# Layer 1's experts as one stream of 71 row slots over all eight batches, in a two-layer attention and expert kernel

## The chip, the core and the metric

The kernel runs on one core of a Trainium2 chip. A core has five engines that run their own instruction lists side by side and wait for each other through semaphores: PE (matrix multiply, with its weight loads shown apart as PEld), DVE (vector), ACT (scalar and activation), POOL (general), and SP, which here only issues DMAs. Work on chip lies in SBUF (128 partitions) and in PSUM, eight banks in which PE leaves its results. The metric is the time of one execution in microseconds, median over the runs.

## The reference, cut to what matters

The input is eight batches of 512 rows of 128 numbers. Each of two layers adds causal attention with 16 heads and then a layer of eight experts:

```
x = x + attention0(layernorm(x))
x = x + experts0(layernorm(x))      # each row goes to 1 of 8 experts
x = x + attention1(layernorm(x))
x = x + experts1(layernorm(x))      # each row goes to 2 of 8 experts

def experts1(x):                    # w1[e]: 128 x 512, w2[e]: 512 x 128
    probs = softmax(x @ gate_w.T + gate_b)
    vals, idx = top_k(probs, 2)
    return sum(vals[k] * (relu(x @ w1[idx[k]] + b1[idx[k]]) @ w2[idx[k]] + b2[idx[k]]) for k in (0, 1))
```

## The kernel before

**Sorted rows and slots.** Rows are not computed with all eight experts. DVE finds for each row its expert and a place in a DRAM table (`route`, `choose`, `places`), POOL sends the rows there by indirect DMAs of one tile of 128 rows each (`scatter`, L1099), and the table is then read in tiles of 128 rows that belong to one expert. Such a tile is a **slot**. For each slot SP loads the expert's `w1` (`fetch_w1`, L943) and the rows (`fetch`), PE turns the rows (`turn_rows`, L1308) and multiplies twice (`first`, L1331, with the ReLU on ACT, and `second`, L1341), and DVE adds the bias into a buffer `kept` (its row reads `w<-psum,w_now`). In layer 1 POOL then sends the finished tile to a DRAM tensor `returned`, each row to the place of its token (`send`, L1107). At the end SP reads `returned` (`take_back`, L997), two loads of 128x512 a batch, since a row has two experts; ahead of the first batch of each group it passes 32 waits, one for each buffer of `kept`, until that half's sends are all done (L992); DVE multiplies them by the gates and adds them to X (`add`, L1555, four instructions of one 128x128 tile each); and SP stores the batch (L1007). Batch 5's adds are on ACT and POOL.

**Groups and halves.** `GROUPS_OF` splits the batches of a layer into groups that are routed together: in layer 1 batches 0 to 3, 4 and 5, 6, and 7. Since experts do not fill their last tile, a table that is closed needs up to 7 slots more than it has tiles of rows. Before the change each half (batches 0 to 3, and 4 to 7) has a table of its own. The first half is one group of 32 + 7 = 39 slots, read in plain order with one DMA for four tiles (L976). The second half is a **stream** of three groups with 9, 8 and 22 slots: a group takes only tiles that are surely full, the last takes the rest, and each tile's place is read from a table `tile_at` at run time, with one DMA a tile (L972). Before the last group's rows are read, the step `tail` (L952) writes eight blocks of empty rows behind the experts' ends. Layer 1 has 78 slots in all.

**Order.** The order of steps on every engine is a table of letters, `ORDERS`, one string an engine, a letter for a kind of step; the PSUM bank of each PE step is a digit of `BANKS`. Attention is split into steps too: `max` (PE L1213 and L1219, then DVE's row maximum, L1524), `score` (PE L1239, the exponential on ACT, and for blocks on the diagonal a mask on POOL, L1088), `values` (L1257). Expert slots and attention steps of the next batches are mixed in these lists. Each engine takes its list strictly in order, so a step that waits holds all behind it. `w1` buffers are a ring of six: SP's load for slot n waits until the `second` of slot n - 6 has been read. The rows' buffers are a ring of two, four tiles each.

## Time and profile before

| | |
|---|---|
| median of 3 runs | 961.92 us (958.96 to 962.04) |
| the profiled execution | 958.88 us |
| its span in the profile | 957.0 us |
| PE busy | 856.2 us |
| PE weight loads busy | 572.6 us |
| DVE busy | 669.4 us |
| ACT busy | 609.4 us |
| POOL busy | 533.2 us |
| TensorE's mean granted clock | 0.963 of full speed |

The span is from the first to the last instruction that the profiler shows; the execution's own time is 1.88 us longer. Busy times overlap, since the engines run side by side; what counts is which engine ends last in each stretch.

### The profile page before, as it was taken

Reading aid. Unit: us, or ns where it says so; the run is one execution under the profiler, and the core shown is the slowest. Engines: PE = TensorE matmul, PEld = TensorE weight load, DVE = VectorE, ACT = ScalarE, POOL = GpSimd, SP = SyncE. Lnnn points to the kernel's source line nnn. Section 1 sums busy time; section 2 is a strip of 40 time slices with the busy share of each in tenths; the row PEclk is TensorE's granted clock in tenths of the full one; section 3 lists DMA queues with packets and bytes.
Section 4 is the critical chain, followed back from the end, with each engine's and each line's share of the span. In section 5 each row is a group of like instructions: output and inputs, shape, how many; then the busy total and the mean of one; then the engine's idle time right before and its main releaser. Section 6 shows DMA issues by size and latency. Waiting matters only on the chain.

```text
span 957.0 us, 24622 instructions
## 1 busy us (share of the span) xinstructions
PE 856.2 (89%) x8968; PEld 572.6 (60%) x8968; DVE 669.4 (70%) x1379; ACT 609.4 (64%) x1173; POOL 533.2 (56%) x809
## 2 busy tenths in 40 slices
PE   3689999989999899988999999999799997899991
PEld 1334455434999445434998444454445597799990
DVE  1889899788545899887567899789999537111117
ACT  3077889865444588685434696788578864555661
POOL 3043544557000588677203787567788775687452
PEclk9999999989999899979999999799899999999996
DMA  5625642444674436341984517435441256778786
GB/s 142 155 83 128 172 112 75 74 113 148 197 223 147 118 113 156 87 135 54 304 255 129 130 54 160 128 78 120 122 124 36 77 167 184 227 228 252 237 247 207
DMA packets 137312, 141.14 MB, mean 147 GB/s; under 512 B 35564, under 2 KB 113452, under 8 KB 137100
## 3 DMA queue, kind: packets, MB, share of 16 engines
q1 hardware_dynamic: 130604, 126.04, 47.4%
q0 software_dynamic: 6592, 13.55, 4.4%
q8 instruction: 74, 1.21, 0.5%
q14 instruction: 42, 0.34, 0.1%
HBM read 98.73 MB, written 44.36 MB: 150 GB/s over the span
## 4 chain that ended last, share of the span: by engine, by line
PE 36%; DVE 9%; issue 3%; DMA 2%; ACT 2%; SPq 0%; POOL 0%; DVEq 0%; ACTq 0%; POOLq 0%
PE psum L1331 11%; PE psum L1341 9%; PE psum L1257 5%; DVE neg_max L1524 4%; PE psum L1239 2%; PE psum L1213 2%; DMA rows_in<-sorted_in 1%; ACT scratch L1453 1%; PE psum L1308 1%; PE psum L1219 1%; PE psum L1283 1%; DVE route L1521 1%; PE psum L1175 1%; DVE X L1555 1%; DMA w<-sorted_out,rows_of 1%
## 5 line engine op out<-in xcount | busy, mean ns | idle before, releaser
L1524 DVE TENSOR_REDUCE neg_max<-psum 128x2 f32<-128x768 f32 (+3 forms) x352 | 379.6, 1119 | 41.0 <-PE psum L1219 38.7
L1453 ACT ACTIVATE scratch<-psum 128x1024 f32<-128x1024 f32 x320 | 316.1, 1022 | 80.4 <-PE psum L1239 77.9
L1088 POOL TENSOR_SCALAR_AFFINE_SELECT scratch<-scratch 128x512 f32<-128x512 f32 x256 | 158.5, 641 | 124.3 <-ACT scratch L1453 123.2
L1331 PE MATMUL psum<-rows_t,w_now 128*128 128x128 f32 x1360 | 169.5, 277 | 5.9 <-issue 3.8
L1257 PE MATMUL psum<-scratch,values 128*32 128x512 f32 (+3 forms) x2048 | 170.0, 452 | 1.7 <-POOL scratch L1088 0.8
L1331 PEld LDWEIGHTS psum<-rows_t,w_now 128*128 128x128 f32 x1360 | 159.7, 193 | 10.4 <-issue 7.4
L1213 PE MATMUL psum<-k_stack,q_stack 52*128 52x128 bf16 (+3 forms) x1024 | 133.2, 321 | 17.8 <-DVE neg_max L1524 7.9
L1341 PE MATMUL psum<-w,hidden_t 128*128 x992 | 131.3, 279 | 5.1 <-ACT hidden_t L1490 1.7
L1239 PE MATMUL psum<-q_stack,k_stack 55*128 55x512 bf16 (+3 forms) x1024 | 121.9, 312 | 12.7 <-DVE neg_max L1524 7.1
L1490 ACT ACTIVATE hidden_t<-psum,w_now 128x128 f32<-128x128 f32 x312 | 88.6, 373 | 60.6 <-PE psum L1331 46.3
L1341 PEld LDWEIGHTS psum<-w,hidden_t 128*128 128x128 f32 x992 | 119.7, 193 | 10.2 <-issue 10.0
L1099 POOL DMA_INDIRECT sorted_in<-xn_half,rows_of x96 | 94.1, 980 | 33.4 <-issue 20.8
L1213 PEld LDWEIGHTS psum<-k_stack,q_stack 52*128 52x128 bf16 x1024 | 43.8, 98 | 96.1 <-issue 39.0
L1521 DVE TENSOR_TENSOR w<-psum,w_now 128x128 f32<-128x128 f32 x78 | 22.7, 291 | 109.1 <-PE psum L1341 107.8
L1107 POOL DMA_INDIRECT returned<-w,goes_to x78 | 76.8, 985 | 37.9 <-issue 19.0
L1219 PE MATMUL psum<-masks_bf 64*128 64x64 bf16 (+2 forms) x1408 | 93.0, 211 | 0.0
L1257 PEld LDWEIGHTS psum<-scratch,values 128*32 128x32 f32 x2048 | 55.1, 111 | 62.1 <-issue 40.6
L1219 PEld LDWEIGHTS psum<-masks_bf 64*128 64x128 bf16 x1408 | 70.6, 101 | 30.9 <-issue 4.9
L1239 PEld LDWEIGHTS psum<-q_stack,k_stack 55*128 55x128 bf16 x1024 | 36.4, 96 | 73.1 <-issue 31.7
L1778 DVE SCALAR_TENSOR_TENSOR hidden_t<-w,psum 128x512 f32<-128x512 f32 x46 | 31.6, 687 | 58.2 <-PE psum L1341 33.0
L1070 POOL TENSOR_TENSOR rot<-rot 128x512 f32<-128x512 f32 x16 | 20.4, 1272 | 50.0 <-DVE rot L1521 49.9
L1078 POOL TENSOR_TENSOR max_parts<-max_rest,max_parts 32x128 bf16<-32x128 f32 x32 | 13.5, 422 | 57.3 <-ACT max_parts L1349 57.1
(141 smaller groups left out, 1007.2 us busy)
## 6 DMA issues: line engine op xcount, KB each, us to landing
w_now<-in_w SPq DMA_DIRECT2D x78, 322.0 KB
w_now<-in_w SPq DMA_DIRECT2D x46, 512.0 KB, 4.4
q_stack<-q_parts SPq DMA_DIRECT2D x64, 192.0 KB, 4.2
q_parts<-q_parts SPq DMA_DIRECT2D x16, 384.0 KB, 2.9
k_stack<-k_parts SPq DMA_DIRECT2D x32, 192.0 KB, 3.7
q_parts<-q_parts SPq DMA_DIRECT2D x16, 256.0 KB, 2.9
w<-in_w SPq DMA_DIRECT2D x16, 256.0 KB, 4.4
scratch<-returned SPq DMA_DIRECT2D x16, 256.0 KB, 4.0
```

Of the source, the lines that this page charges most:

```text
L1088: pool.affine_select(out=diag, in_=diag, compare_op=ALU.is_ge, fill=0.0, base=0, pattern=[[0, 4], [1, P]], channel_multiplier=-1).then_inc ...
L1099: pool.indirect_dma_start(sorted_in[s.layer][half_of(s.layer, g)][:, :], bass.IndirectOffsetOnAxis(ap=row_of(s.layer, g, t, k), axis=0), x ...
L1107: pool.indirect_dma_start(returned[h][:, :], bass.IndirectOffsetOnAxis(ap=goes_to[h][:, j:j + 1], axis=0), kept[slot], None).then_inc(sent ...
L1213: pe.matmul(out[:, j * width:(j + 1) * width], q_stack[i][rows, pair, t * P:(t + 1) * P], k_stack[i][rows, k_of(layer, pair), 0:width], st ...
L1219: ins = pe.matmul(blocks, ident_of[half, :], mask[half, :].unsqueeze(1).to_broadcast([P // 2, n, P // 2]), start=False, stop=(first > widt ...
L1239: ins = pe.matmul(bank[u.bank + k][:, off:off + SEQ - j * P], k_stack[i][rows, k_of(layer, pair), j * P:(j + 1) * P], q_stack[i][rows, pai ...
L1257: ins = pe.matmul(bank[u.bank][CW * c:CW * c + CW, j * P:SEQ], values[batch_of(s) % 3][:, j, col:col + CW], p[:, c % 2, off:off + SEQ - j ...
L1331: ins = pe.matmul(bank[v.bank][:, c * P:(c + 1) * P], w1_now[layer][w.slot][:, n * FFN + c * P:n * FFN + (c + 1) * P], rows)
L1341: ins = pe.matmul(bank[u.bank][:, 0:P], hidden_t[h.slot][:, k * P:(k + 1) * P], w2[layer][:, bass.ds(e, 1), k * DIM:(k + 1) * DIM].rearran ...
L1453: act.activation(expd[s.slot], psum[:, u.bank:u.bank + 2, :], ACT.Exp, scale=SCALE).then_inc(read[u.bank], 1)
L1490: ins = act.activation(hidden_t[s.slot][:, c * P:(c + 1) * P], bank[u.bank][:, c * P:(c + 1) * P], ACT.Relu, bias=w[:, FFN + c:FFN + c + 1])
L1524: return dve.tensor_reduce(out=out, in_=in_, axis=AX, op=op, negate=negate)
```

## The change

All of layer 1 is one stream: the helpers `half_of`/`of_half` give way to `stream_of`, `of_stream` and `same_stream`, which put all four groups of layer 1 in stream 0. The groups now have 25, 16, 8 and 22 slots, 71 in all instead of 78. There is one table `sorted_in` for layer 1, with regions of 8 batches and a tile for each expert, one `returned`, one `goes_to`, `expert_of` and `tile_at`. The first group's rows are now found through `tile_at` too, and only the last group has a tail. The token number that travels with each row gets an offset for the half (L1712 before). The wait of the first `take_back` is for the sends of the whole stream. `rotate` on PE gets an explicit wait. Layer 0 computes and sorts as before. `ORDERS` and `BANKS` are new from the first letter to the last, for all five engines and both layers; the banks of single steps may now be odd ones too.

```diff
     return GROUPS_OF[layer][g][0] // GB
-def of_half(layer, half):
-    return [g for g in range(len(GROUPS_OF[layer])) if half_of(layer, g) == half]
+def stream_of(layer, g):
+    return 0 if layer else half_of(layer, g)
+def of_stream(layer, n):
+    return [g for g in range(len(GROUPS_OF[layer])) if stream_of(layer, g) == n]
+def same_stream(layer, g):
+    return of_stream(layer, stream_of(layer, g))
 def streams(layer, g):
-    return len(of_half(layer, half_of(layer, g))) > 1
+    return len(same_stream(layer, g)) > 1
 def is_final(layer, g):
-    return g == of_half(layer, half_of(layer, g))[-1]
+    return g == same_stream(layer, g)[-1]
 def slots_done(layer, g):
-    tiles = QT * TOPK[layer] * (GROUPS_OF[layer][g][-1] + 1 - half_of(layer, g) * GB)
+    tiles = QT * TOPK[layer] * (GROUPS_OF[layer][g][-1] + 1 - GROUPS_OF[layer][same_stream(layer, g)[0]][0])
     return tiles + (EXPERTS - 1) * (1 if is_final(layer, g) else -1)
 def slots_in(layer, g):
-    same = of_half(layer, half_of(layer, g))
-    return slots_done(layer, g) - (slots_done(layer, g - 1) if g > same[0] else 0)
-def slots_of_half(layer, half):
-    return sum(slots_in(layer, g) for g in of_half(layer, half))
+    return slots_done(layer, g) - (slots_done(layer, g - 1) if g > same_stream(layer, g)[0] else 0)
+def slots_of(layer, n):
+    return sum(slots_in(layer, g) for g in of_stream(layer, n))
 def first_slot(layer, g):
-    return sum(slots_in(layer, k) for k in of_half(layer, half_of(layer, g)) if k < g)
+    return sum(slots_in(layer, k) for k in same_stream(layer, g) if k < g)
 SLOTS = tuple(tuple(slots_in(layer, g) for g in range(len(GROUPS_OF[layer]))) for layer in range(2))
 MAXSLOTS = max(max(ns) for ns in SLOTS)
 HALVES = BATCHES // GB
+STREAMS = (HALVES, 1)
 EPS = 1e-5
 SCALE = float(HD) ** -0.5
 NEG = -3.0e38
...
-C_ID, C_FIRST, C_ONE, C_RANK, C_THR, C_SLOT, C_HALF = 0, 128, 256, 264, 272, 288, 328
-C_TOKEN = 332
+C_ID, C_FIRST, C_ONE, C_RANK, C_THR, C_SLOT = 0, 128, 256, 264, 272, 288
+C_HALF = C_SLOT + MAXSLOTS
+C_TOKEN = C_HALF + QT
...
-RETURNED = 2 * GT * P
-
-REGION = GB * SEQ + P
+RETURNED = HALVES * 2 * GT * P
+
+REGION = BATCHES * SEQ + P
...
 ORDERS = {
...
-        goes_to = [sb(f"goes_to{h}", [P, slots_of_half(1, h)], I32) for h in range(HALVES)]
-        expert_of = [sb(f"expert_of{h}", [1, slots_of_half(1, h)], I32) for h in range(HALVES)]
-        tile_at = sb("tile_at", [1, slots_of_half(1, 1)], I32)
+        goes_to = sb("goes_to", [P, slots_of(1, 0)], I32)
+        expert_of = [[sb(f"expert_of{layer}{n}", [1, slots_of(layer, n)], I32) for n in range(STREAMS[layer])] for layer in range(2)]
+        tile_at = sb("tile_at", [1, slots_of(1, 0)], I32)
...
-        sorted_rows = {(layer, h): EXPERTS * REGION + SPARE * P if len(of_half(layer, h)) > 1 else slots_of_half(layer, h) * P
-                       for layer in range(2) for h in range(HALVES)}
-        sorted_in = [[dram(f"sorted_in{layer}{h}", (sorted_rows[layer, h], widths[layer])) for h in range(HALVES)] for layer in range(2)]
+        sorted_rows = {(layer, n): EXPERTS * REGION + SPARE * P if len(of_stream(layer, n)) > 1 else slots_of(layer, n) * P
+                       for layer in range(2) for n in range(STREAMS[layer])}
+        sorted_in = [[dram(f"sorted_in{layer}{n}", (sorted_rows[layer, n], widths[layer])) for n in range(STREAMS[layer])] for layer in range(2)]
-        returned = [dram(f"returned{h}", (RETURNED + slots_of_half(1, h) * P, DIM)) for h in range(HALVES)]
+        returned = dram("returned", (RETURNED + slots_of(1, 0) * P, DIM))
...
                             sp.wait_ge(tails_set, EXPERTS * DMA)
-                        tiles = sorted_in[s.layer][half_of(s.layer, s.b)].rearrange("(n p) d -> n p d", p=P)
+                        tiles = sorted_in[s.layer][stream_of(s.layer, s.b)].rearrange("(n p) d -> n p d", p=P)
                         found = values_at(tile_at, first_slot(s.layer, s.b) + 4 * s.x, n, EXPERTS * REGION_TILES + SPARE - 1)
...
-                        for slot, value in enumerate(sends_made(of_half(1, half_of(1, g))[-1])):
+                        for slot, value in enumerate(sends_made(same_stream(1, g)[-1])):
-                        first = (k * GT + QT * x) * P
-                        sp.dma_start(taken_back(b, k), returned[half_of(1, g)][first:first + QT * P, :].rearrange("(p t) d -> p t d", p=P)
+                        first = ((2 * half_of(1, g) + k) * GT + QT * x) * P
+                        sp.dma_start(taken_back(b, k), returned[first:first + QT * P, :].rearrange("(p t) d -> p t d", p=P)
...
-                    pool.indirect_dma_start(sorted_in[s.layer][half_of(s.layer, g)][:, :], bass.IndirectOffsetOnAxis(ap=row_of(s.layer, g, t, k), axis=0),
+                    pool.indirect_dma_start(sorted_in[s.layer][stream_of(s.layer, g)][:, :], bass.IndirectOffsetOnAxis(ap=row_of(s.layer, g, t, k), axis=0),
-                    h, j = half_of(1, g), first_slot(1, g) + s.x
-                    pool.indirect_dma_start(returned[h][:, :], bass.IndirectOffsetOnAxis(ap=goes_to[h][:, j:j + 1], axis=0),
+                    j = first_slot(1, g) + s.x
+                    pool.indirect_dma_start(returned[:, :], bass.IndirectOffsetOnAxis(ap=goes_to[:, j:j + 1], axis=0),
...
                 elif s.kind == "rotate":
+                    x = of("turn", 1, b, "xn")
+                    pe.wait_ge(read[x.uses[0].bank], x.uses[0].after)
                     room(u)
                     pe.matmul(bank[u.bank], (wq1, wq1_sw)[s.y][:, :], xt[of("turn", 1, b, "xn").slot][:, :]).then_inc(full[u.bank], 1)
 
...
-                        dve.tensor_copy(xn_half[:, mine, DIM], consts[:, C_TOKEN + mine.start:C_TOKEN + mine.stop])
+                        dve.tensor_scalar(xn_half[:, mine, DIM], consts[:, C_TOKEN + mine.start:C_TOKEN + mine.stop],
+                                          float(half_of(1, g) * 2 * GT * P), None, ALU.add, ALU.bypass)
...
-                        base, ends = (region if g == of_half(layer, half_of(layer, g))[0] else e_small[:, 4, :]), e_small[:, 3, :]
+                        base, ends = (region if g == same_stream(layer, g)[0] else e_small[:, 4, :]), e_small[:, 3, :]
...
-                    dve.tensor_copy(expert_of[half_of(layer, g)][:, j:j + ns], slot_f[:, 0:ns]).then_inc(experts_known, 1)
+                    dve.tensor_copy(expert_of[layer][stream_of(layer, g)][:, j:j + ns], slot_f[:, 0:ns]).then_inc(experts_known, 1)
```

Three places of the new orders follow; in each the first list is before the change, the second after it. Line numbers after the change are 10 to 13 higher.

**PE at the start.** L1145, L1153, L1159 and L1161 (after: L1155 to L1171) are the turn, q and k/v products of one batch; L1213 and L1219 (L1225 and L1231) begin batch 0's row maxima.

```order
L1145 MATMUL psum<-consts,xn 128x128 x4
L1153 MATMUL psum<-xn_t,wq 128x512
L1159 MATMUL psum<-xn_t,wkv 32x128 x4
L1161 MATMUL psum<-wkv,xn_t 128x32 x4
L1213 MATMUL psum<-k_stack,q_stack 128x128 x8
L1219 MATMUL psum<-masks_bf 128x4x64 x4
L1213 MATMUL psum<-k_stack,q_stack 128x256 x4
L1219 MATMUL psum<-masks_bf 128x2x64 x4
```

```order
L1155 MATMUL psum<-consts,xn 128x128 x4
L1163 MATMUL psum<-xn_t,wq 128x512
L1169 MATMUL psum<-xn_t,wkv 32x128 x4
L1171 MATMUL psum<-wkv,xn_t 128x32 x4
L1155 MATMUL psum<-consts,xn 128x128 x4
L1163 MATMUL psum<-xn_t,wq 128x512
L1169 MATMUL psum<-xn_t,wkv 32x128 x4
L1171 MATMUL psum<-wkv,xn_t 128x32 x4
L1225 MATMUL psum<-k_stack,q_stack 128x128 x8
L1231 MATMUL psum<-masks_bf 128x4x64 x4
```

Batch 2's turn and products now stand ahead of the first row maximum; before, two batches did.

**POOL in the attention of batch 7.** AFFINE_SELECT (L1088, after: L1098) is the mask of a score block; the DMA to `sorted_in` (L1099, after: L1109) scatters rows of layer 1's group 1, the DMA to `returned` (L1107, after: L1117) sends a finished tile of group 0. The last AFFINE_SELECT of each list is the last of batch 7.

```order
L1088 AFFINE_SELECT scratch<-scratch 128x4x128 x9
L1099 DMA sorted_in<-xn_half,rows_of 18304x129 x2
L1088 AFFINE_SELECT scratch<-scratch 128x4x128 x4
L1043 TENSOR_TENSOR ln_small<-ln_small,consts 128x4
L1044 TENSOR_TENSOR ln_small<-ln_small,consts 128x4
L1046 TENSOR_TENSOR ln_small<-ln_small,consts 128x4
L1048 TENSOR_TENSOR ln_small<-ln_small 128x4
L1088 AFFINE_SELECT scratch<-scratch 128x4x128 x3
```

```order
L1109 DMA sorted_in<-xn_half,rows_of 34688x129
L1098 AFFINE_SELECT scratch<-scratch 128x4x128
L1117 DMA returned<-w_0,goes_to 17280x128 x2
L1042 TENSOR_TENSOR route_small<-consts 128x4
L1109 DMA sorted_in<-xn_half,rows_of 34688x129
L1117 DMA returned<-w_0,goes_to 17280x128
L1098 AFFINE_SELECT scratch<-scratch 128x4x128 x2
L1109 DMA sorted_in<-xn_half,rows_of 34688x129 x2
L1098 AFFINE_SELECT scratch<-scratch 128x4x128
```

Before, two scatters of group 1 stood ahead of the last masks. Now, with rows ahead of those shown, 11 scatters and 5 sends stand between group 1's first scatter and the last mask.

**DVE at the end.** w2_0<-psum,w1_now (L1521, after: L1533) takes a finished slot out of PSUM; the SCALAR_TENSOR_TENSOR of L1555 (after: L1567) is `add`, and its gate names the half and the expert of the two, `gate01` the first half's second.

```order
L1555 SCALAR_TENSOR_TENSOR X<-scratch,gate00,X 128x128 x4
L1521 TENSOR_TENSOR w2_0<-psum,w1_now 128x128
L1555 SCALAR_TENSOR_TENSOR X<-scratch,gate01,X 128x128 x4
L1555 SCALAR_TENSOR_TENSOR X<-scratch,gate00,X 128x128 x4
L1555 SCALAR_TENSOR_TENSOR X<-scratch,gate01,X 128x128 x4
L1555 SCALAR_TENSOR_TENSOR X<-scratch,gate00,X 128x128 x4
L1555 SCALAR_TENSOR_TENSOR X<-scratch,gate01,X 128x128 x4
L1555 SCALAR_TENSOR_TENSOR X<-scratch,gate00,X 128x128 x4
L1555 SCALAR_TENSOR_TENSOR X<-scratch,gate01,X 128x128 x4
L1555 SCALAR_TENSOR_TENSOR X<-scratch,gate10,X 128x128 x4
L1555 SCALAR_TENSOR_TENSOR X<-scratch,gate11,X 128x128 x4
```

```order
L1533 TENSOR_TENSOR w2_0<-psum,w1_now 128x128 x13
L1567 SCALAR_TENSOR_TENSOR X<-scratch,gate00,X 128x128 x4
L1567 SCALAR_TENSOR_TENSOR X<-scratch,gate01,X 128x128 x4
L1567 SCALAR_TENSOR_TENSOR X<-scratch,gate00,X 128x128 x4
L1567 SCALAR_TENSOR_TENSOR X<-scratch,gate01,X 128x128 x4
L1567 SCALAR_TENSOR_TENSOR X<-scratch,gate00,X 128x128 x4
L1567 SCALAR_TENSOR_TENSOR X<-scratch,gate10,X 128x128 x4
L1567 SCALAR_TENSOR_TENSOR X<-scratch,gate01,X 128x128 x4
L1567 SCALAR_TENSOR_TENSOR X<-scratch,gate00,X 128x128 x4
L1567 SCALAR_TENSOR_TENSOR X<-scratch,gate10,X 128x128 x8
L1567 SCALAR_TENSOR_TENSOR X<-scratch,gate11,X 128x128 x8
L1567 SCALAR_TENSOR_TENSOR X<-scratch,gate01,X 128x128 x4
L1567 SCALAR_TENSOR_TENSOR X<-scratch,gate11,X 128x128 x4
```

Before, one add stood ahead of the last slot and the adds followed in the order of batches, 14 in all. Now all 14 stand behind the last slot, and the sixth, the first with `gate10`, is batch 6's. On SP all sixteen loads of L997 (after: L1007) now stand behind the last load of a `w1`, by order of batch; before, the first half's eight were issued by themselves, two of them ahead of the last two `w1`.

## Rows read from the trace of the kernel before

**Rows 1.** The page of the run before: span and PE

```profile
span 957.0 us, 24622 instructions
...
PE 856.2 (89%) x8968; PEld 572.6 (60%) x8968; DVE 669.4 (70%) x1379; ACT 609.4 (64%) x1173; POOL 533.2 (56%) x809
```

**Rows 2.** Windows: busy us of PE, PEld, DVE, ACT, POOL; clock, DMA share, GB/s

```profile
675.00:700.00 25.00, 19.92 (x247) 11.05 (x240) 24.16 (x34) 12.14 (x18) 18.98 (x24) 0.86 0.57 157
775.00:850.00 75.00, 65.39 (x538) 62.22 (x537) 30.97 (x151) 40.45 (x136) 51.35 (x73) 0.98 0.70 210
840.00:920.00 80.00, 77.48 (x673) 75.43 (x672) 13.87 (x51) 50.23 (x171) 52.86 (x75) 1.00 0.78 232
```

**Rows 3.** Matmuls of three lines from 840 to 920 us, ns min/median/max

```profile
L1331 PE MATMUL psum<-rows_t,w_now x317: 275/275/349, 840.3 to 920.0; 128*128 128x128 f32 x159
...
L1341 PE MATMUL psum<-w,hidden_t x317: 274/275/372, 839.8 to 919.2; 128*128 x159
...
L1308 PE MATMUL psum<-consts,rows_in x39: 272/273/300, 849.4 to 919.4; 128*128 128x128 f32 x39
```

**Rows 4.** The chain from 934 us to the end: start, us, what

```profile
937.35 2.43 DMA returned<-w,goes_to
...
940.57 0.32 SPq L997
...
941.88 0.43 SPq L997
...
943.73 0.32 SPq L997
...
944.10 3.15 DMA scratch<-returned
...
953.23 0.52 DVE X L1555 x2
```

**Rows 5.** The timeline from 930 us: start, us, instruction

```profile
935.11 1.15 PE L1341 MATMUL psum<-w,hidden_t 128*128 x8 [0.42 <-ACT hidden_t L1490]
...
936.50 10.29 DVE L1555 SCALAR_TENSOR_TENSOR X<-scratch,gate,X 128x128 f32<-128x128 f32 x36
```

**Rows 6.** The timeline of PE, ACT and DVE in the first 60 us

```profile
19.36 1.11 PE L1145 MATMUL psum<-consts,xn 128*128 128x128 f32 x4 [2.06 <-ACT xn L1412]
...
23.77 1.92 PE L1161 MATMUL psum<-wkv,xn_t 128*128 128x32 f32 x8
27.98 0.61 PE L1213 MATMUL psum<-k_stack,q_stack 52*128 52x128 bf16 x8 [2.29 <-issue]
...
17.67 1.64 ACT L1412 ACTIVATE xn<-X,ln_small 128x128 f32<-128x128 f32 x4
...
23.29 0.60 ACT L1349 ACTIVATE q_parts<-psum 128x512 bf16<-128x512 f32 x1 [2.18 <-PE psum L1153]
...
49.76 0.85 DVE L1579 BATCH_NORM_STATS2 ln_small<-X 128x6 f32<-128x128 f32 x4
50.64 0.38 DVE L1582 BATCH_NORM_AGGREGATE ln_small<-ln_small 128x2 f32<-128x6 f32 x4
```

**Rows 7.** The timeline of DVE in the routing of layer 1's group 1

```profile
748.33 0.48 DVE L1753 SCALAR_TENSOR_TENSOR jump<-taken,e_small 1x8 f32<-1x8 f32 x1
...
750.97 0.22 DVE L1524 TENSOR_REDUCE route<-route 1x9 f32<-1x72 bf16 x1
```

**Rows 8.** The timeline of POOL, two indirect DMAs four apart

```profile
764.31 1.00 POOL L1099 DMA_INDIRECT sorted_in<-xn_half,rows_of  x1 [0.16 <-issue]
...
769.62 1.00 POOL L1099 DMA_INDIRECT sorted_in<-xn_half,rows_of  x1 [0.16 <-issue]
```

**Rows 9.** The timeline of SP and DVE: tail step and one row fetch

```profile
819.89 10.20 SPq L952 DMA_DIRECT2D sorted_in<-in_empty_rows  x8
...
897.36 2.23 SPq L972 DMA_DIRECT2D rows_in<-sorted_in  x4
...
902.16 0.35 DVE L1538 CAST goes_to<-rows_in 128x4 int32<-128x4 f32 x1 [1.37 <-DMA rows_in<-sorted_in]
```

92 lines of the change are left out of this document (46 added, 46 removed).

## The prediction

> **What bounds the kernel now.** I read the page first: PE is busy 856.2 of a span of 957.0 us [rows 1]. Such an average mixes stages, so the windows come next [rows 2]. From 675 to 700 us, in layer 1's attention, DVE is busy 24.16 of 25 us and PE 19.92: the row maxima and the routing end last there. From 840 to 920 us only expert slots run: PE is busy 77.48 of 80 us, its weight loads 75.43, DVE 13.87 and POOL 52.86, so PE alone bounds it. Between them, from 775 to 850 us, PE is idle 75.00 - 65.39 = 9.61 us while the last groups are routed. Last, the chain and the timeline of the end: the last matmuls begin at 935.11 and take 1.15 us [rows 5], so PE ends at 936.26 and 20.7 us of the span follow with PE idle. There the order is last send, 32 waits, take-back, add, store [rows 4]. The kernel is thus bound by three things in turn, and the change touches each.
>
> **The slots that are gone.** From 840 to 920 us the trace has 317 + 317 matmul instructions of L1331 and L1341 [rows 3]. A slot has eight of each (four products, each in two passes), so this is 634 / 16 = 39.6 slots, or 80 / 39.6 = 2.02 us a slot, with its share of turned rows (39 tiles, L1308). Seven slots less are 7 x 2.02 = 14.1 us. They are PE's full price only where PE ends last; all of layer 1's slots but the first few lie in such stretches, so I take 14.1. ACT, DVE, POOL (seven sends) and SP (seven loads of w1) lose work too, which lay beside PE's: nothing for it. The bound from below, if half of it fell in a stage where PE waits for others, is 7.0.
>
> **The end.** I count from L, the landing of the last send. Before, L is 937.35 + 2.43 = 939.78, that is 3.5 us after PE's end [rows 4, 5]. Nothing changes up to there: POOL's last sixteen sends follow their slots one by one in both orders.
> Before, the first half's adds ran while the last send was under way: DVE did 36 instructions in 10.29 us from 936.50 [rows 5], 0.286 us each, 1.14 us an add. Only 32 semaphore waits, four loads, 32 waits again and batch 6's load stand between L and the rest: the first load is issued at 940.57 (0.8 after L), the fourth ends at 942.31, so a load costs SP 0.44 to 0.47; 32 waits take until 943.73, 1.4 us; that load lands at 944.10 + 3.15 = 947.25 [rows 4].
> After, all adds wait for L, since the one `returned` is complete only then. SP: rest of the waits 1.1 (25 instead of 18 of the 32 stand behind the last one), eight loads 3.7, waits 1.4, four loads 1.8, waits 1.4: batch 6's first load is issued at L + 9.4 and lands 3.5 later, at L + 12.9. DVE begins at about L + 4.6 and would have done five adds by L + 10.3, but its sixth is batch 6's: it stands still for 2.6 us. Then nine adds are left, 9 x 1.14 = 10.3, to L + 23.2. The last store takes as now, from 953.75 (the end of the last add) to 957.0, 3.3 us [rows 1, 4]. The end is at L + 26.5 instead of L + 17.2: **+9.3 us**. If DVE's sixth add cost no wait it would be +6.7; if the transfers (16 loads and 8 stores of 256 KB, 6.3 MB) ran at the mean 232 GB/s of the slot stage [rows 2] they would take 27 us instead of the 22 that I give them, so +14.
>
> **The start.** PE's list has batch 2's turn and products ahead of the first row maximum. For batch 1 this group runs from 19.36 to 23.77 + 1.92 = 25.69, 6.3 us. Batch 2's needs its normalised rows; ACT makes them in 1.64 us behind the q copy that ends at 23.89, so at 25.5. PE would reach the first maximum at about 32.0 instead of 27.98 [rows 6]: +4.0. DVE's list in turn has the statistics of batches 2, 3 and 4 ahead of the maxima, in its idle time; each costs 0.85 + 0.38 = 1.2 us now inside the stretch of maxima [rows 6], so -3.7. PE's 6.3 us for batch 2 are also not due later. I take 0 for the start: between +4.0 (nothing paid back) and -2.3 (both engines' work is worth its full length: 4.0 - 6.3).
>
> **Routing group 0 as a stream.** The extra operations are those of group 1 now: from 748.33 to 750.97, 2.6 us of small instructions on DVE [rows 7]; the others replace such as are dropped. For group 0 they fall in the stage that DVE bounds, where a stall of DVE makes the next maximum late and with it PE. Between 0 (a wait for PE near by swallows it) and 2.6, I take 1.4. The offset of the token and PE's new wait cost nothing: the first is one small instruction instead of another, the second waits for a copy that the latent product of the same batch waits for.
>
> **Row fetches and fills.** Group 0's rows now take four DMAs a fetch and a load of table entries: SP spends 2.23 us on four [rows 9] where one DMA of 256 KB stood. SP is mostly idle in that stage; 0. Five fills of the old padding slots fall away, in DMA time that nothing waits for; 0. The eight tail DMAs, 10.20 us on SP [rows 9], are there before and after, once each, with w1 loads behind them.
>
> **Sum.** -14.1 + 9.3 + 0 + 1.4 = -3.4 us. Against the profiled execution's own 958.88 us this is 955.5. The median of the runs shown is 961.92, 3.0 above that execution, and the sum does not depend on which of them is taken: **958.5 us** for the median. All other parts of the lists are new as well, in both attentions; of these I can't price single moves, and they carry the width of the range. What a measurement can't tell from no change is about 0.3%, 2.9 us: 959.0 to 964.8.
>
> **The rivals.**
> (a) *The re-ordered attention is better packed* (0.17). DVE and PE start the maxima with batch 2's work done, and both bounds of the start hold in full: -2.3, and DVE's added routing falls into a wait, 0. With the end at +6.7: -14.1 + 6.7 - 2.3 = -9.7, 952.2 us. For it: PE idles anyway between 25.69 and 27.98 [rows 6]; against it: a stretch like that of 675 to 700 is already full on DVE [rows 2].
> (b) *POOL makes batch 7's masks late*, the slower side (0.20). Between group 1's first scatter and batch 7's last mask POOL had 2 indirect DMAs and now has 16. Four indirect DMAs take 769.62 - 764.31 = 5.3 us, 1.33 each [rows 8]; 14 more are 18.6 us. What covers it is PE's own list: batch 7's last product now has 14 slots ahead instead of 5, 9 x 2.02 = 18.2 us of PE work. Cover and delay are equal, so any slot that comes late shows. It decides (slower by more than 2.9) once 6.3 us of the 18.6 are uncovered; with half of them, -3.4 + 9.3 = +5.9, 967.8 us. One would see PE wait on POOL's `scratch` in the values of batch 7.
> (c) *Rows come late* (0.18). Fewer slots stand between the last routing and its first rows, 24 instead of 39, and the first `turn_rows` of group 3 only 16 slots, 32 us, behind its `places`. The fetch at 897.36 landed by 902.16, 4.8 us [rows 9]; in three places the new PE list leaves only four to five products of 0.9 us between a freed row buffer and the next turn from it. Each may stall 1 to 2 us: -3.4 + 4 = +0.6, 962.5 us. The Trainium skill (DMA: Bandwidth & Descriptors, Bandwidth) speaks against single tiles too: it says to batch DMAs to 1 MiB or more and gives 0.95 us for 64 KB. By this page four tiles occupy the DMA engines for 3.8 us, an estimate from its figure, which in a stage where they are busy 0.78 of the time would make rows later still; no run here shows a 64 KB transfer alone.
> (d) *The slots bring less*: with -7.0 for them, +3.7, 965.6 us; part of (b) in its effect, and small (0.05).
>
> **How the numbers follow.** My forecast has 0.40, with a range of its own from 954.5 to 962 (the bounds 0 to 2.6, -2.3 to +4.0 and the end's +6.7 to +14 don't all go one way). Faster by over 0.3%: (a) and 0.31 of the forecast's 0.40, together 0.48. Within: 0.09 of the forecast, (c), and little of (b): 0.29. Slower: most of (b), (d): 0.23. The range takes in (a) with some room, and (b)'s half-covered case: 950 to 968.
>
> **What would show it.** Right: 14 x 8 fewer matmul instructions on the two slot lines; PE's last matmul some 12 us earlier, near 924; after it 30 us with PE idle, in them DVE waiting about 2.6 us behind its fifth add for a load, and 56 add instructions behind the last slot; the first maximum at 32 us. Wrong: the first matmul of group 0 at another distance from the end of layer 0 than now, which would be the attention's lists; PE waits on POOL masks late in batch 7 (b); waits of L1320 on rows (c); loads landing at less than 300 GB/s in the end, which would make it DMA's and not DVE's.

## The result: the change makes the kernel slower

984.54 us median (980.74 to 990.64, 4 runs) stand against 961.98 before (4 runs): a ratio of 1.0256, 95% interval [1.0209, 1.0303]. I had forecast 958.5 us in a range of 950 to 968. The profiled execution took 990.64 us, the longest of the four, so its trace shows some 6 us more loss than the median.

First the page of the changed kernel (span, busy time, granted clock by slices, one group):

```profile
span 988.6 us, 24399 instructions
...
PE 862.2 (87%) x8849; PEld 572.1 (58%) x8849; DVE 672.0 (68%) x1381; ACT 601.9 (61%) x1143; POOL 525.1 (53%) x792
...
PEclk9999999998999989999999999998898999979995
...
L1343 PE MATMUL psum<-rows_t,w_now 128*128 128x128 f32 x1304 | 168.0, 283 | 14.2 <-DMA w_now<-in_w 12.3
```

119 matmuls are gone, 17 for each of the seven slots (8968 before, [rows 1]), and PE is still 6 us longer busy. Then windows of the changed kernel: window, length, busy us of each engine (instructions), clock, DMA share, GB/s:

```profile
0.00:50.00 50.00, 31.19 (x205) 17.86 (x207) 25.47 (x67) 17.95 (x44) 15.83 (x37) 1.00 0.69 154
675.00:700.00 25.00, 20.74 (x207) 8.39 (x205) 23.52 (x57) 17.00 (x23) 15.21 (x21) 0.84 0.62 143
840.00:920.00 80.00, 64.38 (x489) 61.47 (x490) 15.02 (x66) 34.77 (x117) 47.19 (x66) 0.91 0.68 194
845.00:895.00 50.00, 37.92 (x270) 36.19 (x270) 7.40 (x33) 19.20 (x66) 26.80 (x37) 0.86 0.65 185
```

The third row answers to the last of [rows 2]: the stretch in which PE alone was the bound (77.48 of 80 us) has lost 13 us of PE's work. What PE waits for shows in its waits over the whole span (us in total, times, longest):

```profile
PE psum L1343 <- DMA w_now<-in_w: 12.3, 7, 3.6
...
PE psum L1251 <- DMA q_stack<-max_parts_out: 10.1, 7, 2.8
...
PE psum L1320 <- DMA rows_in<-sorted_in: 4.5, 3, 2.9
```

L1251 are the scores of attention, which wait for the row maxima on their way through DRAM. In the kernel before, the same list has no wait of the first two kinds, and 0.3 us of the third. Behind the first stands SP's queue. Its timeline in group 1's slots (start, us from first to last issue, line, count):

```profile
842.97 5.84 SPq L982 DMA_DIRECT2D rows_in<-sorted_in  x8
849.04 3.45 SPq L953 DMA_DIRECT2D w_now<-in_w  x3
853.65 1.88 SPq L982 DMA_DIRECT2D rows_in<-sorted_in  x4
855.72 1.17 SPq L953 DMA_DIRECT2D w_now<-in_w  x2
858.09 5.31 SPq L982 DMA_DIRECT2D rows_in<-sorted_in  x8
864.67 1.37 SPq L953 DMA_DIRECT2D w_now<-in_w  x3
866.90 9.74 SPq L962 DMA_DIRECT2D sorted_in<-in_empty_rows  x8
```

Last the end, to be read against [rows 4, 5]: last products, last send, loads, and the adds of DVE:

```profile
956.28 1.15 PE L1353 MATMUL psum<-w,hidden_t 128*128 x8 [0.43 <-ACT hidden_t L1502]
...
958.52 0.96 POOL L1117 DMA_INDIRECT returned<-w,goes_to  x1 [0.58 <-issue]
961.11 10.09 SPq L1007 DMA_DIRECT2D scratch<-returned  x16
964.44 2.38 DVE L1567 SCALAR_TENSOR_TENSOR X<-scratch,gate,X 128x128 f32<-128x128 f32 x8 [6.68 <-DMA scratch<-returned]
...
973.61 11.62 DVE L1567 SCALAR_TENSOR_TENSOR X<-scratch,gate,X 128x128 f32<-128x128 f32 x36 [3.08 <-DMA scratch<-returned]
```

PE ends at 957.43 and 31.2 us follow; I had said 30. DVE stands still once more, 3.08 us (I had said 2.6).

To see where the rest went I matched PE's matmuls with the steps of its list and took the end of the same step in each profile; for a slot this is the end of its first product (`first`). This is worked out from the trace's records, not a view of it. Slots are numbered 0 to 70 in the new order; the seven that are gone stood between slots 31 and 32. The columns between the first and the last are kernels of the experiments below:

```
end of the step, us           before  old_lists  start_new  cut_250  cut_380_again  front_new   after
first row maximum, batch 0      29.0       29.2       32.9     32.7           33.0       32.8    32.8
layer 0, group 0, slot 22      305.9      304.5      307.9    309.2          314.8      318.9   318.3
layer 0, group 1, slot 22      522.1      518.8      523.2    521.1          533.9      540.6   538.8
layer 1, slot 0                756.0      754.5      763.4    758.1          769.6      781.3   771.1
slot 16                        801.8      803.1      809.3    804.8          817.9      827.2   821.3
slot 31                        841.4      848.4      852.0    850.1          861.0      871.6   862.2
slot 41                        874.9      869.8      875.4    873.0          883.7      894.0   895.5
last product                   936.3      931.4      936.8    934.4          945.0      955.3   957.4
end of the span                957.0      959.8      966.2    962.3          972.9      983.2   988.6
```

The changed kernel's 31.6 us are thus: 15.1 up to slot 0 (both attentions and layer 0), 5.7 more to slot 31, -0.2 to slot 41 (where seven slots less should have given 10 or more), 0.6 behind it, and 10.5 at the end. One profile each stands behind these numbers. Through layer 0 PE, ACT, DVE and POOL have the same lists in before and in old_lists, and still the two differ by 1.4 and 3.3 us in the two rows of layer 0, so a difference of 3 us in one row says little. The sign that I had named for a loss in attention, another distance from the end of layer 0 to slot 0, looks at the wrong place: it is 233.9 us before and 232.3 after. The loss is already there at the end of layer 0, 16.7 us against before and 20.0 against old_lists.

### The profile page after: what moved, and what is told of

Its sections match the earlier page's. It is cut to its first block, busy times and chain, and to the rows that moved or that the text cites. A ratio compares the mean times of both kernels' runs of the same rounds, so it can differ in the third digit from the quotient of the medians.

```text
span 988.6 us, 24399 instructions
## 1 busy us (share of the span) xinstructions
PE 862.2 (87%) x8849; PEld 572.1 (58%) x8849; DVE 672.0 (68%) x1381; ACT 601.9 (61%) x1143; POOL 525.1 (53%) x792
## 4 chain that ended last, share of the span: by engine, by line
PE 45%; DVE 16%; DMA 11%; issue 8%; POOL 7%; SPq 7%; ACT 6%; DVEq 0%; ACTq 0%; POOLq 0%
PE psum L1343 11%; DVE neg_max L1536 9%; PE psum L1353 8%; PE psum L1269 7%; PE psum L1225 4%; PE psum L1251 4%; ACT scratch L1465 4%; DMA rows_in<-sorted_in 2%; DMA max_parts_out<-max_parts 2%; SPq L982 2%; POOL scratch L1098 2%; DMA w_now<-in_w 2%; POOL sorted_in L1109 2%; DMA q_stack<-max_parts_out 2%; PE psum L1231 1%
## 5 line engine op out<-in xcount | busy, mean ns | idle before, releaser
L1098 POOL TENSOR_SCALAR_AFFINE_SELECT scratch<-scratch 128x512 f32<-128x512 f32 x256 | 160.0, 644 | 173.9 <-ACT scratch L1465 173.0
L1343 PE MATMUL psum<-rows_t,w_now 128*128 128x128 f32 x1304 | 168.0, 283 | 14.2 <-DMA w_now<-in_w 12.3
L1269 PE MATMUL psum<-scratch,values 128*32 128x512 f32 (+3 forms) x2048 | 174.6, 462 | 2.9 <-POOL scratch L1098 1.1
L1343 PEld LDWEIGHTS psum<-rows_t,w_now 128*128 128x128 f32 x1304 | 157.2, 197 | 20.6 <-issue 10.2
L1225 PE MATMUL psum<-k_stack,q_stack 52*128 52x128 bf16 (+3 forms) x1024 | 132.2, 320 | 19.1 <-DVE neg_max L1536 9.3
L1251 PE MATMUL psum<-q_stack,k_stack 55*128 55x512 bf16 (+3 forms) x1024 | 119.9, 311 | 19.5 <-DMA q_stack<-max_parts_out 10.1
L1353 PE MATMUL psum<-w,hidden_t 128*128 x936 | 126.9, 286 | 5.7 <-ACT w L1361 3.0
L1353 PEld LDWEIGHTS psum<-w,hidden_t 128*128 128x128 f32 x936 | 116.7, 199 | 11.2 <-issue 10.4
L1502 ACT ACTIVATE hidden_t<-psum,w_now 128x128 f32<-128x128 f32 x284 | 80.4, 373 | 62.2 <-PE psum L1353 37.9
L1109 POOL DMA_INDIRECT sorted_in<-xn_half,rows_of x96 | 94.1, 980 | 32.1 <-issue 20.6
L1117 POOL DMA_INDIRECT returned<-w,goes_to x71 | 69.6, 980 | 47.7 <-DVE w L1533 29.8
L1231 PE MATMUL psum<-masks_bf 64*128 64x64 bf16 (+2 forms) x1408 | 92.4, 210 | 0.0
L1225 PEld LDWEIGHTS psum<-k_stack,q_stack 52*128 52x128 bf16 x1024 | 43.0, 97 | 84.0 <-issue 28.8
L1231 PEld LDWEIGHTS psum<-masks_bf 64*128 64x128 bf16 x1408 | 70.4, 100 | 31.6 <-issue 7.0
L1251 PEld LDWEIGHTS psum<-q_stack,k_stack 55*128 55x128 bf16 x1024 | 37.3, 96 | 85.6 <-issue 26.1
L1533 DVE TENSOR_TENSOR w<-psum,w_now 128x128 f32<-128x128 f32 x71 | 20.0, 289 | 83.2 <-PE psum L1353 83.2
L1088 POOL TENSOR_TENSOR max_parts<-max_rest,max_parts 32x128 bf16<-32x128 f32 x32 | 13.4, 420 | 70.6 <-ACT max_parts L1361 70.3
L1493 ACT ACTIVATE w<-psum 128x512 f32<-128x512 f32 x46 | 27.4, 595 | 29.1 <-DVE hidden_t L1791 18.6
```

The source lines that it names most:

```text
L1098: pool.affine_select(out=diag, in_=diag, compare_op=ALU.is_ge, fill=0.0, base=0, pattern=[[0, 4], [1, P]], channel_multiplier=-1).then_inc ...
L1109: pool.indirect_dma_start(sorted_in[s.layer][stream_of(s.layer, g)][:, :], bass.IndirectOffsetOnAxis(ap=row_of(s.layer, g, t, k), axis=0), ...
L1117: pool.indirect_dma_start(returned[:, :], bass.IndirectOffsetOnAxis(ap=goes_to[:, j:j + 1], axis=0), kept[slot], None).then_inc(sent_back[ ...
L1225: pe.matmul(out[:, j * width:(j + 1) * width], q_stack[i][rows, pair, t * P:(t + 1) * P], k_stack[i][rows, k_of(layer, pair), 0:width], st ...
L1231: ins = pe.matmul(blocks, ident_of[half, :], mask[half, :].unsqueeze(1).to_broadcast([P // 2, n, P // 2]), start=False, stop=(first > widt ...
L1251: ins = pe.matmul(bank[u.bank + k][:, off:off + SEQ - j * P], k_stack[i][rows, k_of(layer, pair), j * P:(j + 1) * P], q_stack[i][rows, pai ...
```

## Experiments

The program of the change and its lists of steps can be parted: the lists of before, with the seven slots taken out, drive the new program as well. All kernels were timed beside the kernel before on the same chip.

**1 to 3. Program or lists?** PE's list begins so in the two:

```diff
 ORDERS["pe"], after -> old_lists
-&ef&ef&efjjjjj&jjjjjjj&ljjjjjjjjpppjjjppljjp...
+&ef&efjjjjjjjjjjjjjljjjjjjjjjppppppjjlj&jjpep...
```

> The program of the change (one stream of 71 slots, one taking back at the end) with the lists and banks of the kernel before: seven slots of the first half's end are left out of them, its taking back and adds are moved behind the last slot in the order of the batches, everything else stands where it stood. Nothing of the computation changes. Theory A, the new lists are what costs: the stretch up to the last slot is as before less seven slots (-14), the end is as in the changed kernel or somewhat longer (+9 to +12), so 956 to 962 us. Rival B, the stream itself costs (all row fetches of group 1 by address on SP, w1 late behind them): the 16 to 18 us that the changed kernel loses between 845 and 895 us show here too, 972 to 980 us. Rival C, both by halves: 963 to 971 us.

> The changed kernel with the old lists (and banks) for all steps that the kernel before had done by 560 us: layer 0 with its experts, and layer 1's attention up to the scores of batch 2. Behind that stand the new lists. Theory A1, the first part of the lists loses what the milestones show there (first product +7, last slots of layer 0 +15 to +17): 968 to 971 us. Rival A2, what the front loses is waited away later, behind the experts' weights and rows: 978 to 984 us.

> The other half of the exchange: the new lists for all steps that the changed kernel had done by 577 us, and behind them the old lists less seven slots, with the taking back and the adds at the end. Theory A1 with additive parts: old_lists plus 13 to 16 us, so 970 to 977 us. Rival A2, the front's delay is hidden later: within 4 us of old_lists. Rival B, the stream on SP costs whatever the lists: 980 us or more.

Measured: old_lists 962.77 us, 1.0036 [0.9995, 1.0078]; front_old 976.86, 1.0144 [1.0069, 1.0219]; front_new 985.11, 1.0242 [1.0158, 1.0326]. The one stream with the old lists costs or gives nothing that can be told; the new lists cost the rest, about 22 us at the medians. The parts don't add: the new first part alone costs all of it, the new second part alone 14. Once the first part is new, the second parts are level in the table (the changed kernel begins its slots 10 us earlier than front_new and takes 12 us longer for them). So neither A1 nor A2 stands as I wrote it. The 985.11 lies where rival B of front_new put it, but old_lists rules B out: the same stream on SP is there too.

**4. A cheaper tail step under the new lists.**

```diff
-                        at = sp.value_load(ends_at[0:1, e:e + 1], ...)
+                        if e % LOADED == 0:
+                            found = values_at(ends_at, e, LOADED, EXPERTS * REGION - P)
+                        at = found[e % LOADED]
```

> The changed kernel, with the eight addresses of the tail step taken by two loads of four values in place of eight loads of one. In the profile of the changed kernel that step holds SP for 9.7 us (1.2 us for each of its eight transfers); two loads at 1.0 us and eight issues at 0.5 us make it 6 us. Theory S, SP bounds the stretch from 840 to 895 us: -3 to -4 us, so 980 to 982 us, and the PE's waits for w1 in 866 to 884 us go from 6.6 to under 4 us. Rival, SP's queue isn't the bound there: no change, 983 to 986 us.

Measured: 986.84 us, 1.0226 [1.0138, 1.0314]: no gain. In its timeline the step is as much shorter as meant, but PE's waits between 845 and 915 us have only changed their name:

```profile
866.20 6.01 SPq L964 DMA_DIRECT2D sorted_in<-in_empty_rows  x8
```

```profile
PE psum L1322 <- DVE w L1535: 7.7, 2, 5.6
PE psum L1345 <- DMA w_now<-in_w: 4.1, 4, 3.2
PE psum L1322 <- DMA rows_in<-sorted_in: 1.9, 1, 1.9
```

L1322 is `turn_rows`: rows are late where weights were. By the chain SP waits there for the last scatter's landing, until 880.5 us, with all its loads behind it. That this is the cause was read, not tried.

**5. The tail step spread, with the old lists.** In old_lists PE loses 5.7 us between slots 16 and 31 (1.3 behind before, then 7.0). SP's timeline, of before and then of old_lists, and a wait of PE in old_lists between 797 and 860 us:

```profile
817.24 0.42 SPq L976 DMA_DIRECT2D rows_in<-sorted_in  x1
```

```profile
816.31 1.88 SPq L982 DMA_DIRECT2D rows_in<-sorted_in  x4
...
826.70 9.80 SPq L962 DMA_DIRECT2D sorted_in<-in_empty_rows  x8
```

```profile
PE psum L1343 <- DMA w_now<-in_w: 4.4, 1, 4.4
```

Four tiles by address cost SP 1.9 us, and 0.9 for the load of their addresses (tail_two's chain), where one transfer of 0.4 us stood. The tail step starts 6.8 us later than in before ([rows 9]: 819.89), and the weights behind it are late. The wait is not all new: at the same place PE stood 3.0 us in before, with no releaser in the profile. Of the 5.7 us 3.6 are waiting (10.3 us from slot 16 to slot 31 instead of 6.7) and the rest longer matmuls, 9.1 us of them at the lower granted clock instead of 3.4.

```diff
+                if tails and s.kind == "fetch_w1" and s.x % 2:
+                    set_tail(sorted_in[1][0])      # one load, one transfer
```

> The one-stream program with the lists of before (old_lists), and the tail step's eight loads and transfers no longer in one piece: one of them goes ahead of every second fetch of w1. SP issues as much as it did, only not all at once. In old_lists that step holds SP for 9.8 us from 826.7 us, w1 lands late behind it (PE waits 4.4 us at L1343) and slots 25 to 28 lose 5.7 us against before. Theory S, SP is where the stream loses: 4 to 6 us less than old_lists, so 957 to 959 us, and that wait goes. Rival, another wait stands behind it (rows of group 1): 961 to 963 us.

Measured: 965.53 us, 1.0076 [1.0047, 1.0106]: no gain, and above what both theories gave. Its profile is of the fastest run (960.76). Slot 31 comes 4.9 us earlier there than in old_lists (843.5), slot 41 not at all (869.9).

**6. Less issued, not only spread.** old_two has the edits of experiments 5 and 4 together.

> old_spread (the one-stream program with the lists of before, the tail step's transfers one ahead of each second fetch of w1), and now with the eight addresses of that step taken by two loads of four values. Spreading alone moved PE's waits about and left slot 41 where it was: the sum of what SP issues was the same. This takes about 4 us of it away between 826 and 862 us. Theory S, in group 1's slots the sum of SP's issues is the bound: PE 3 to 4 us earlier from slot 41 on than in old_spread, so 960 to 962 us. Rival, the sum isn't the bound, the rows of the last batches are: as old_spread, 964 to 966 us.

> old_two once more (the one-stream program with the lists of before, the tail step spread, its addresses by two loads); its first run fell in the hour in which every kernel took 8% longer, and stood at 1.0082 of before. Theory S, the sum of SP's issues is the bound in group 1's slots: PE 3 to 4 us earlier than old_lists from slot 41 on, 959 to 962 us. Rival: as old_lists and old_spread, 963 to 966 us.

Measured: 1.0082 [1.0045, 1.0119] in the first run, where before took 1040.67 us; then 960.41 us beside 959.46, 1.0023 [0.9996, 1.0050]. In its profile slot 41 ends at 865.3, 4.6 us earlier than in old_spread, and the last product at 926.8 (931.2). From slot 16 to slot 41 it takes 61.7 us, old_spread 65.5 and old_lists 66.7. That speaks for theory S, that what SP no longer issues comes back, and the two ratios, 1.0076 and 1.0023, are apart as well. Two things hold it back. Against old_lists no gain shows in the times: 0.9 us above before in both, and the profile of old_two_again is that of its fastest run (956.39). And SP is not issuing all the time: between 826 and 870 us it waits 7.7 us for others there, 8.4 in old_spread and 6.7 in old_lists. So the sum of SP's issues is a large part of the bound in these slots; that it is all of it isn't shown.

**7 to 9. Where do the new lists lose?** start_new, cut_250 and cut_380 take the new lists up to 60, 246 and 380 us; front_new did up to 577.

> old_lists, with the new lists for what the changed kernel had done by 60 us and the old ones behind: only the start is new (batch 2's turn, products and copies ahead of the first maxima). My prediction priced the start at 0 between -2.3 and +4.0. If it is 0: 961 to 964 us. If the first maxima's 3.8 us are never made good: 966 to 967 us. If the start alone carries the loss of the front: 975 us or more.

> old_lists, with the new lists for what the changed kernel had done by 246 us (attention of the first four batches) and the old ones behind. In front_new, where the new lists reach to 577 us, PE stood some 10 us behind old_lists at this point by equal work, and 18 to 24 us at 577 us. Theory, the loss is made before the experts of group 0 and kept: 972 to 976 us. Rival, it is made in layer 0's experts and the attention beside them (250 to 577 us): 962 to 966 us. Rival, the joint itself costs: 980 us or more.

> old_lists, with the new lists for what the changed kernel had done by 380 us and the old ones behind. New lists up to 246 us cost 3 us, up to 577 us 22 us. Theory, many small waits, spread over the stretch: +6 to +13 us over cut_250, so 972 to 979 us. Rival A, one place before 380 us makes all of it: 983 us or more. Rival B, one place behind it (layer 0's group 1 and its experts): 965 to 969 us.

> cut_380 once more, for the same reason. Theory of many small waits: 972 to 979 us; one place ahead of 380 us: 983 us or more; one place behind it: 965 to 969 us.

Measured: start_new 966.70 us, 1.0065 [1.0043, 1.0088]; cut_250 966.23, 1.0071 [1.0043, 1.0100]; cut_380 1.0149 [1.0091, 1.0207] beside the 1040.67, then 979.57, 1.0221 [1.0172, 1.0270]. The start costs about 4 us by the medians of start_new and old_lists, 3 by their ratios (the intervals just overlap), and is not made good; the attention of the first four batches adds nothing to it; the great part, near 19 us by front_new, is made between 250 and 577 us. cut_380 lies in the middle, but its profile has 5 us of waiting near 375 us where its two lists join, so it does not tell many small waits from one place cleanly. Windows of cut_250 and then of front_new:

```profile
245.00:270.00 25.00, 25.00 (x222) 24.26 (x221) 12.12 (x19) 9.42 (x19) 2.17 (x5) 1.00 0.73 216
...
345.00:370.00 25.00, 24.12 (x278) 13.61 (x274) 22.45 (x52) 21.66 (x35) 21.74 (x36) 1.00 0.57 141
```

```profile
245.00:270.00 25.00, 22.31 (x181) 20.61 (x180) 13.95 (x25) 7.56 (x18) 2.39 (x6) 0.86 0.58 185
...
345.00:370.00 25.00, 22.74 (x227) 11.34 (x229) 19.49 (x32) 17.99 (x31) 20.29 (x31) 0.86 0.15 48
```

PE is busy 2.7 and 1.4 us less in these windows of front_new, and their granted clock is 0.86 instead of 1.00. The same time is not the same work in the two, so the rows show only that the two go together. The kind of wait that grows is that of the scores for the maxima's way through DRAM; over the whole span, cut_250 and then front_new:

```profile
PE psum L1251 <- DMA q_stack<-max_parts_out: 5.5, 3, 3.0
```

```profile
PE psum L1251 <- DMA q_stack<-max_parts_out: 10.1, 6, 3.3
```

These 4.6 us are a small part of the 19, and cut_250's own 5.5 (start_new has 1.1) cost nothing that shows in its time. How the rest comes about stands under "What the waits set off".

**10 and 11. The end by itself.** before_late moves the first half's loads, adds and stores behind the last slot in the kernel before. before_wait also lets them wait for the last send of all:

```diff
-                        for slot, value in enumerate(sends_made(of_half(1, half_of(1, g))[-1])):
+                        for slot, value in enumerate(sends_made(len(SLOTS[1]) - 1)):
```

> The kernel before (two streams, 78 slots, its own lists), only that the first half's rows are taken back, added and stored behind the last slot, with the other half's. My prediction put the end at +9.3 us for this; the profiles showed +7.8 (old_lists) and +10.5 us (the changed kernel) between PE's last product and the end. Theory, the end is that price by itself: 969 to 972 us. Rival, the first half's loads and adds also cost PE something where they stood, and their leaving gives it back: 963 to 967 us.

> before_late (two streams, the first half taken back behind the last slot; 959 us), and now the first half's taking back also waits for the last send of all, as it must in one stream. Theory E, the end of one stream is dear since all sixteen transfers start only when the last send has landed, not since sixteen adds stand there: +6 to +8 us over before_late, so 965 to 967 us, and 28 us between PE's last product and the end in place of 21. Rival, the adds' place alone: within 2 us of before_late.

> before_wait once more, for the same reason. Theory E: 965 to 967 us (6 to 8 over before_late), 28 us between PE's last product and the end. Rival: within 2 us of before_late (959).

Measured: before_late 958.95 us, 0.9984 [0.9963, 1.0006], far from my 969 to 972; before_wait 1.0104 [1.0034, 1.0174] beside the 1040.67, then 965.54 us, 1.0065 [1.0045, 1.0085], as theory E said. Loads and adds in before_late, then in before_wait_again:

```profile
924.13 18.60 SPq L997 DMA_DIRECT2D scratch<-returned  x16
...
933.06 18.20 DVE L1555 SCALAR_TENSOR_TENSOR X<-scratch,gate,X 128x128 f32<-128x128 f32 x56
```

```profile
945.51 10.48 SPq L997 DMA_DIRECT2D scratch<-returned  x16
948.88 18.16 DVE L1555 SCALAR_TENSOR_TENSOR X<-scratch,gate,X 128x128 f32<-128x128 f32 x56 [7.19 <-DMA scratch<-returned]
```

The 56 instructions take 18.2 us in both. In the first the rows are there when the last slot leaves (PE ends at 932.8, 21.2 us follow); in the second DVE stands 7.2 us for the first load (PE ends at 941.4, 28.4 follow). The end of one stream is dear through what the transfers wait for, not through the number of adds behind the last slot.

**12. The spread tail step under the new lists.**

> The changed kernel with the tail step's transfers spread: one ahead of each fetch of w1, what is left ahead of the last group's first fetch of rows. In the changed kernel slots 32 to 41 lose 11 to 12 us against old_lists. Theory S as in old_spread (the sum of SP's issues binds, not their place): no change beyond 3 us, 982 to 987 us. Rival, the block of 9.7 us itself makes those slots late: 973 to 978 us.

> new_spread once more: in its first run every kernel, the kernel before too, took 8% longer, and it stood at 1.0076 of before. Theory P, the block of the tail step is what makes slots 32 to 41 late under the new lists: 972 to 979 us, 8 to 12 us less than after_again. Theory S, only the sum of SP's issues counts: within 3 us of after_again.

> The changed kernel once more, as the measure for new_spread on the same chip and hour: 981 to 988 us where before takes 960 to 962.

Measured: new_spread 1.0076 [1.0045, 1.0106] beside the 1040.67, with no run of the changed kernel in that hour; then 993.84 us, 1.0322 [1.0267, 1.0376], beside after_again with 986.58, 1.0256 [1.0210, 1.0302]. Spreading alone is no gain here either; P is wrong. It is 7 us worse at the medians, with intervals that overlap (1.0267 to 1.0302), so neither a loss nor theory S's "within 3 us" is shown. What makes slots 32 to 41 late under the new lists stays open: neither this nor experiment 4 brought them back.

**13. A version that beats both.** Two streams, the first half's adds behind the last slot, the tail step spread and its addresses by two loads:

> before_late (two streams, the first half taken back behind the last slot; 959.0 us) with the same two edits of the tail step: a candidate to beat both kernels. There SP has slack, since the first 39 slots' rows come by one transfer for four slots, so if only the sum of SP's issues binds, nothing is gained: 957 to 960 us. If the block of 10.2 us itself is waited for (slot 28 comes 8.1 us after slot 27 in the profile of before, where its neighbours stand 1 to 5 us apart), 954 to 957 us.

Measured: 954.04 us (952.32 to 954.31), 0.9943 [0.9922, 0.9963]: 5.4 us faster than before, 30 faster than the change. Slot 28 comes 4.9 us behind slot 27 (8.1 in before, 6.9 in before_late, which is the kernel to compare with), and slot 31 comes 3.3 us earlier than in before_late. That fits the expectation that the block itself was waited for, and the 954 to 957 us given for it. But the kernel has both edits, the spreading and the cheaper addresses, and neither was tried alone with two streams, so how much each gave isn't shown.

## Why the prediction was wrong, by its own steps

- **The lists: "of these I can't price single moves, and they carry the width of the range".** This is the step that failed. I let them widen the range by a few us to both sides; they cost about 22 (old_lists against the changed kernel), nearly all of the result. Against old_lists 20.0 us of it are there at the end of layer 0, in lists that the prediction left out of its sum. [Rows 2] could have bounded them on one side: with DVE busy 24.16 of 25 us a new order has little to win there, and each new wait to lose.
- **The start: 0, bounds -2.3 and +4.0.** Measured 3 to 4 (start_new). The mechanism was right (first maximum at 32.8, I had said 32.0); "paid back" was wrong.
- **Row fetches and fills: 0, "SP is mostly idle in that stage".** Measured 5.7 us with the old lists, between slots 16 and 31 (one profile each; 3.6 of them waiting). I took SP's idle share over the stage, though [rows 9] shows a step of 10.20 us there with the weights behind it. I had counted this step as the same before and after, and not asked what is late when SP reaches it 6.8 us later.
- **Seven slots: -14.1.** From slot 31 to slot 32 before took 15.3 us and old_lists 4.4: 10.9; by slot 41 old_lists has gone from 7.0 us behind before to 5.1 ahead, 12.1. The kind is right, the size 2 to 3 us too large; 2.02 us a slot was a mean over a stretch. That is rival (d), at less than half of its size.
- **The end: +9.3.** +7.8 in old_lists (28.5 us behind the last product instead of 20.7), +7.2 in before_wait_again against before_late, +10.5 in the changed kernel. This step held, with its working. What I believed after it, that adds behind the last slot are dear by themselves, fell with before_late.
- **Routing group 0: +1.4, between 0 and 2.6.** PE's wait for DVE behind this routing shows it, before and then old_lists:

```profile
679.49 0.40 PE L1227 MATMUL psum<-consts,neg_max 128*32 128x128 f32 x1 [3.47 <-DVE neg_max L1524]
```

```profile
679.10 0.40 PE L1239 MATMUL psum<-consts,neg_max 128*32 128x128 f32 x1 [6.27 <-DVE neg_max L1536]
```

  The wait is 2.8 us longer (and 6.3 us again in start_new, old_spread and old_two_again): the mechanism was right, the cost at or just over the upper bound. The changed kernel, whose order differs, has no such wait there.
- **Rival (a), attention better packed:** the contrary; its lists are what cost, and 0.48 for "faster" was far too much. **Rival (b), POOL late with batch 7's masks:** not so in the changed kernel; PE's waits for POOL's `scratch` are 1.1 us in its whole span. old_lists has one such wait of 2.62 us, which is nearly all that it loses between slots 0 and 16 (1.5 us ahead of before, then 1.3 behind):

```profile
764.78 1.50 PE L1269 MATMUL psum<-scratch,values 128*32 128x384 f32 x24 [2.62 <-POOL scratch L1098]
```

  POOL itself stood 5.55 us for DVE's `ln_small` ahead of it, so it was not POOL's DMAs that came late.
- **Rival (c), rows late:** there, 4.5 us in three waits, and too small to decide. For w_now, 12.3 us, I had no rival. The Trainium skill (DMA: Bandwidth & Descriptors, Bandwidth), named with (c), speaks against single tiles and pointed the right way. No run here shows a 64 KB transfer alone; the price that the traces show is SP's time, 2.8 us in place of 0.4.

**What the waits set off.** old_lists and the changed kernel run the same 8849 matmuls. PE is busy 842.3 us in the one and 862.2 in the other, and ends 26.1 us later: 19.9 of these are busy time and 6 waiting. The granted clock fell with it: 0.963 in the profiled run of before, 0.958 in old_lists, 0.948 in the changed kernel. The trace records each stretch at the lower level, 1.2 instead of 2.4 GHz. PE was busy for 46.5 us of such stretches in old_lists and for 72.1 in the changed kernel. There two matmuls of L1343 that follow each other start 213 ns apart at the lower level and 112 at the upper (medians, worked out from the records), so about half of that time is lost: 12.8 of the 19.9 us. Between cut_250 and front_new this is nearly all: PE is busy 15.1 us longer (846.5 and 861.6), 47.9 and 78.2 us of it at the lower level, and half of the difference is 15.2; the other 5.8 us of its later end are waiting. What such a stretch does is seen in tail_two, where eight products of L1345 take 1.95 us behind 3.17 us without work, and 1.13 behind 0.64:

```profile
867.28 1.95 PE L1345 MATMUL psum<-rows_t,w_now 128*128 128x128 f32 x8 [3.17 <-DMA w_now<-in_w]
...
903.93 1.13 PE L1345 MATMUL psum<-rows_t,w_now 128*128 128x128 f32 x8 [0.64 <-DMA w_now<-in_w]
```

Windows about the two; the third number from the end is the clock:

```profile
867.00:869.30 2.30, 2.02 (x10) 2.05 (x11) 0.00 (x0) 0.00 (x0) 0.00 (x0) 0.58 0.93 328
903.90:905.10 1.20, 1.17 (x10) 1.20 (x11) 0.00 (x0) 1.12 (x4) 0.72 (x1) 1.00 0.98 322
```

Among the changed kernel's own runs the fastest, 980.74 us, had a clock of 0.957 and the slowest, 990.64, had 0.948. That the waits bring the stretches about is read from this going together; no run moved the clock alone. Where the other 7 us of longer matmuls in the changed kernel come from stays open, and so does which moves between 250 and 577 us begin it all.

## What to carry to other kernels

When a change brings new lists of steps, price it in two, the program with the old lists and the lists: here the first was level and the second cost 22 us. A queue that issues the weights' loads must be summed over its stretch, and the question is what comes late if a step on it starts later. Spreading a long step alone gave nothing here (old_spread, new_spread); spread and with fewer address loads it gave some 4 us in the kernel of two streams (before_late_two against before_late). Work behind the last product is cheap if its data can be there already, and costs a whole round trip if it waits for the last piece.

## What the runs showed of the hardware

- A PE that waits more was also slower while it worked: 20 us more busy time for the same matmuls at 6 us more waiting (changed kernel against old_lists), 12.8 of the 20 by the lower clock. Matmuls of L1343 started 112 ns apart at the upper level and 213 at the lower.
- A load of one address and its transfer took SP 1.2 us; with four addresses to a load, 0.75 (9.74 and 6.01 us for eight).
- The same chip ran the kernel before at 961.87 us in one hour and at 1040.67 in another. There PE's waits with no releaser in the profile were 23.8 us on one line (before_wait's first run), against 0.3 in the profile of before:

```profile
PE psum L1341 <- issue: 23.8, 7, 11.1
```

What these waits are stays open. Only kernels run side by side in such an hour can be compared, and even their ratios move (new_spread: 1.0076 there, 1.0322 in another hour on another chip).
